# A spectral-MLP stage with its mask products on VectorE and its MLP blocks, sums and transform slots in another order

## The reference

```python
residual = x
xn = _ln(transpose(x, (0, 2, 3, 1)), ln1w, ln1b)          # layer norm over the 64 channels
xf = jnp.fft.rfft2(xn, axes=(1, 2), norm='ortho')
o1r, o1i = relu(complex product of xf with w1 + b1)
o2r, o2i = complex product of (o1r, o1i) with w2 + b2
mask = ((jnp.abs(o2r) > THR) | (jnp.abs(o2i) > THR)).astype(o2r.dtype)
o2r, o2i = o2r * mask, o2i * mask                          # THR = 0.01
x = residual + irfft2(complex(o2r, o2i))
h = gelu(_ln(x, ln2w, ln2b) @ mw1 + mb1, approximate=False)   # 64 -> 256
x = x + (h @ mw2 + mb2)                                    # 256 -> 64
```

## Time and profile before

| | |
|---|---|
| median of 3 runs | 3960.04 us (3946.08 to 3962.07) |
| profiled execution | 3955.85 us, of which the span of instructions 3953.8 us |
| TensorE busy | 3359.4 us (85%) |
| VectorE busy | 2409.8 us (61%) |
| ScalarE busy | 2378.0 us (60%) |
| GpSimd busy | 1706.6 us (43%) |
| mean granted TensorE clock | 0.937 |

### The profile page before, as it was taken

The page is one execution under the profiler, slowest core; times in us unless marked ns, Lnnn a source line. Parts: engine busy times, 40 slices in busy tenths (PEclk is TensorE's granted clock), DMA queues, the critical chain, the costliest instruction groups (busy, mean ns, idle before and its releaser), DMA issues. The chain is left out here.

```text
span 3953.8 us, 54117 instructions
## 1 busy us (share of the span) xinstructions
PE 3359.4 (85%) x18664; PEld 2064.3 (52%) x18664; DVE 2409.8 (61%) x4175; ACT 2378.0 (60%) x3944; POOL 1706.6 (43%) x1397
## 2 busy tenths in 40 slices
PE   2952779999999999898989899999999999967579
PEld 0741646555555556464646464656464646345237
DVE  1834566656565666666666666565756565449567
ACT  0843466656565656576766565665656565637448
POOL 2404444544444444444454545545444443234242
PEclk9975889999999999999999999999999999989879
DMA  9861111101111111212111101010111111163698
GB/s 222 257 223 60 38 48 43 59 27 59 42 45 43 44 49 43 86 65 107 65 66 43 59 28 59 27 64 26 60 38 49 38 49 43 64 237 123 165 276 242
DMA packets 235118, 334.15 MB, mean 85 GB/s; under 512 B 38625, under 2 KB 163681, under 8 KB 228721
## 3 DMA queue, kind: packets, MB, share of 16 engines
q1 hardware_dynamic: 198112, 298.44, 22.2%
q10 hardware_dynamic: 28784, 18.44, 2.0%
q0 software_dynamic: 7968, 13.99, 1.4%
HBM read 183.99 MB, written 146.80 MB: 84 GB/s over the span
## 5 line engine op out<-in xcount | busy, mean ns | idle before, releaser
L1490 ACT ACTIVATE a_hidden<-a_wide,a_up_b 128x1024 f32<-128x1024 f32 x512 | 569.4, 1112 | 168.7 <-PE a_wide L1657 168.7
L1657 PE MATMUL a_wide<-a_yc,a_up_fold 64*128 64x512 f32 x2048 | 587.7, 649 | 45.1 <-ACT a_hidden L1490 40.8
L1668 PE MATMUL a_result<-a_hidden,a_down 128*64 128x512 f32 x2048 | 513.4, 623 | 72.2 <-DVE a_x L1356 72.2
L1252 POOL TENSOR_TENSOR a_y<-a_o,a_mag 128x256 f32<-128x256 f32 (+1 forms) x512 | 362.0, 732 | 424.0 <-DVE a_mag L1345 424.0
L1210 POOL TENSOR_TENSOR a_y<-a_x,a_stat 128x512 f32<-128x512 f32 x256 | 266.6, 1044 | 349.7 <-DVEq L1388 320.8
L1328 DVE TENSOR_TENSOR a_o<-a_bank,a_mix_b 128x512 f32<-128x512 f32 (+1 forms) x272 | 181.6, 668 | 376.9 <-PE a_bank L1614 372.3
L1356 DVE TENSOR_TENSOR a_x<-a_result,a_x 128x512 f32<-128x512 f32 x256 | 176.3, 689 | 339.3 <-PE a_result L1683 337.1
L1632 PEld LDWEIGHTS a_bank<-a_dft_h,a_g 128*128 128x128 f32 x2080 | 285.6, 200 | 175.5 <-issue 115.3
L1647 PE MATMUL a_bank<-a_dft_hi,a_y 128*128 128x128 f32 x2048 | 280.1, 303 | 70.5 <-POOL a_y L1252 70.5
L1614 PEld LDWEIGHTS a_bank<-a_mix,a_o 128*128 128x128 f32 x2080 | 253.9, 192 | 154.7 <-issue 135.8
L1632 PE MATMUL a_bank<-a_dft_h,a_g 128*128 128x128 f32 x2080 | 290.4, 284 | 47.3 <-DVE a_g L1321 47.3
(11 more groups left out here) (189 smaller groups left out, 6359.6 us busy)
## 6 DMA issues: line engine op xcount, KB each, us to landing
a_x<-rows SPq DMA_DIRECT2D x112, 512.0 KB, 4.4
rows<-a_x SPq DMA_DIRECT2D x112, 512.0 KB, 2.9
box_x<-in_x SPq DMA_DIRECT2D x64, 256.0 KB, 4.3
turned<-box_o SPq DMA_DIRECT2D x64, 256.0 KB, 3.7
a_y<-turned SPq DMA_DIRECT2D x16, 1024.0 KB, 11.5
box_x<-rows SPq DMA_DIRECT2D x16, 1024.0 KB, 24.2
turned<-box_work SPq DMA_DIRECT2D x64, 256.0 KB, 2.0
box_x<-turned SPq DMA_DIRECT2D x64, 256.0 KB, 3.9
```

The lines of the kernel that those rows point to most:

```text
L1252: ins = G.tensor_tensor(y[n % 2][:, :, to].rearrange("p c k -> p k c"), o2[:, j % 3, lo:4, r], mask[:, lo:4], ALU.mult)
L1490: A(hidden[:, i % 2, j], wide[:], ACT.Gelu, bias=up_b2[:, l, j:j + 1]).then_inc(s_hid, 1)
L1657: mm = M(wide[:, half * BANK:(half + 1) * BANK], up_fold[cs, l, j * P:(j + 1) * P], yc[cs, i % 2], start=True, stop=True)
L1668: mm = M(result[half * C:(half + 1) * C, :], down[:, l, j, :], hidden[:, i % 2, j, half * BANK:(half + 1) * BANK], start=j == 0, stop=j == ...
```

## The change

1. **Mask products.** `masked` and `spectrum` on GpSimd are gone. VectorE's `masks` keeps the maximum, drops the comparison as an instruction of its own, and multiplies `o2` by `(top > THR)` in `scalar_tensor_tensor` instructions, two for each chunk, written to `y`. `o2` has two buffers in place of three.
2. **MLP order.** `turn_back` writes `turned`, and the residual reads `turned`, so `result` belongs to `mlp_down` alone; `mlp_down` is cut into its two halves, which stand in two places of the quarter and wait for `mlp_delta` of the block before (`s_delta`). `turn` comes later in a quarter but for a block further on (Q + 2 in place of Q + 1), so it waits for `normalise` of Q + 2 and for the residual of Q - 2. ScalarE's `operand` becomes the first thing of its quarter; the squares come after the second slot's part.
3. **Slots.** `REST_SLOTS` 5, 7, 17, 18 become 3, 9, 17, 18; `BACKWARD_SLOT` 43 becomes 44; `NEXT_SLOTS` 47, 48, 51, 53 become 48, 49, 53, 57.
4. **Sums.** In quarter 5 the pair of reductions and the root move from the second slot to the fourth, behind the end of the forward transform.
5. **GpSimd's long operations.** `next_y` of quarter 10 is written a slot later.

```diff
-REST_SLOTS = (5, 7, 17, 18)
-FORWARD_SLOT, SPECTRUM_SLOT, BACKWARD_SLOT = 19, 23, 43
-NEXT_SLOTS = (47, 48, 51, 53)
+REST_SLOTS = (3, 9, 17, 18)
+FORWARD_SLOT, SPECTRUM_SLOT, BACKWARD_SLOT = 19, 23, 44
+NEXT_SLOTS = (48, 49, 53, 57)
...
-        o2 = sb("o2", [P, 3, 4, 2, C])
+        o2 = sb("o2", [P, 2, 4, 2, C])
...
-                def masked(n, j):
-                    before, mask = N_CHUNK * n, mag[:, j % 2, :, 0]
-                    kw, lo = first_kw(j), 1 if j < 2 else 0
-                    pool.wait_ge(s_top, 2 * (before + j + 1))
-                    if j < 2:
-                        ins = G.tensor_tensor(ends[:, 1 - j], o2[:, j % 3, 0], mask[:, 0:1].broadcast_to([P, 2, C]), ALU.mult)
-                    if j > 0:
-                        for r in range(2):
-                            to = slice(r * HALF + kw + lo, r * HALF + kw + 4)
-                            ins = G.tensor_tensor(y[n % 2][:, :, to].rearrange("p c k -> p k c"), o2[:, j % 3, lo:4, r],
-                                                  mask[:, lo:4], ALU.mult)
-                    ins.then_inc(s_masked, 1)
...
                     for s in range(4):
-                        parts(n, q, s, inverse, other, spectrum, other)
+                        parts(n, q, s, inverse, other, other, other)
                         if s == 0 and 0 <= Q + 2 < BLOCKS * RUNS:
                             normalise(Q + 2)
-                        if s in (0, 2) and comes:
+                        late = 1 if q == 10 else 0
+                        if s - late in (0, 2) and comes:
...
                     V.tensor_tensor(top[:, 0:k], top[:, 0:k], mag[:, j % 2, 0:k, 1], ALU.max).then_inc(s_top, 1)
-                    dve.wait_ge(s_top, 2 * (before + j) + 1)
-                    V.tensor_scalar(top[:, 0:k], top[:, 0:k], THR, None, ALU.is_gt).then_inc(s_top, 1)
+                    dve.wait_ge(s_top, before + j + 1)
+                    if j < 2:
+                        ins = V.scalar_tensor_tensor(
+                            out=ends[:, 1 - j], in0=top[:, 0:1].broadcast_to([P, 2, C]), scalar=THR,
+                            in1=o2[:, j % 2, 0], op0=ALU.is_gt, op1=ALU.mult)
+                    if j > 0:
+                        for r in range(2):
+                            to = slice(r * HALF + kw + lo, r * HALF + kw + 4)
+                            ins = V.scalar_tensor_tensor(
+                                out=y[n % 2][:, :, to].rearrange("p c k -> p k c"), in0=top[:, lo:4], scalar=THR,
+                                in1=o2[:, j % 2, lo:4, r], op0=ALU.is_gt, op1=ALU.mult)
+                    ins.then_inc(s_masked, 1)
...
-                    V.tensor_tensor(x[:, row:row + HB], rows(result), x[:, row:row + HB], ALU.add).then_inc(s_res, 1)
+                    V.tensor_tensor(x[:, row:row + HB], rows(turned), x[:, row:row + HB], ALU.add).then_inc(s_res, 1)
...
-                    parts(n, q, 1, inverse, forward, spectrum, backward)
-                    for strip in strips_at(n, q):
-                        sum_up(*strip)
-                    if q % 4 == 1 and FIRST_ROOT <= r < END_ROOT:
-                        root(r)
-                    for s in range(2, 4):
+                    for s in range(1, 4):
                         parts(n, q, s, inverse, forward, spectrum, backward)
+                        if s == (3 if q == 5 else 1):
+                            for strip in strips_at(n, q):
+                                sum_up(*strip)
+                            if q % 4 == 1 and FIRST_ROOT <= r < END_ROOT:
+                                root(r)
...
+                    if 0 <= Q + 1 < BLOCKS * RUNS:
+                        operand(Q + 1)
                     if mlp:
                         gelu(Q, 0)
...
                     parts(n, q, 0, inverse, forward, spectrum, backward)
-                    if 0 <= Q + 1 < BLOCKS * RUNS:
-                        operand(Q + 1)
                     parts(n, q, 0, other, other, magnitude, other)
+                    parts(n, q, 1, inverse, forward, spectrum, backward)
                     for strip in strips_at(n, q):
                         square(*strip)
-                    parts(n, q, 1, inverse, forward, spectrum, backward)
...
-                def mlp_down(i):
+                def mlp_down(i, j):
                     l = layer_of(i // BLOCKS)
-                    pe.wait_ge(s_hid, HC * (i + 1))
+                    pe.wait_ge(s_hid, HC * i + j + 1)
                     if i:
-                        pe.wait_ge(s_res, i)
-                    for j in range(HC):
-                        for half in range(2):
+                        pe.wait_ge(s_delta, i)
+                    for half in range(2):
...
                     if i:
                         pe.wait_ge(s_yc, i)
+                    if i >= 4:
+                        pe.wait_ge(s_res, i - 3)
...
                 def turn_back(i):
                     pe.wait_ge(s_delta, i + 1)
+                    pe.wait_ge(s_yc, min(i + 4, BLOCKS * RUNS))
+                    if i + 4 > BLOCKS * RUNS:
+                        pe.wait_ge(s_res, i)
...
-                    if 0 <= Q + 1 < BLOCKS * RUNS:
-                        turn(Q + 1)
+                    if 0 <= Q - 1 < BLOCKS * RUNS:
+                        mlp_down(Q - 1, 0)
                     parts(n, q, 1, inverse, forward, spectrum, backward)
                     if mlp:
                         mlp_up(Q, 1)
                     parts(n, q, 2, inverse, forward, spectrum, backward)
                     if 0 <= Q - 1 < BLOCKS * RUNS:
-                        mlp_down(Q - 1)
+                        mlp_down(Q - 1, 1)
+                    if 0 <= Q + 2 < BLOCKS * RUNS:
+                        turn(Q + 2)
```

More of the change, by code:

```diff
@@ L1325, in spectrum @@
                         dve.wait_ge(s_mix2, before + j + 1)
-                        if j >= 3:
-                            dve.wait_ge(s_masked, before + j - 2)
-                        V.tensor_tensor(o2[:, j % 3, 0:k].rearrange("p k r c -> p k (r c)"), four(bank[3])[:, 0:k],
+                        if j >= 2:
+                            dve.wait_ge(s_masked, before + j - 1)
+                        V.tensor_tensor(o2[:, j % 2, 0:k].rearrange("p k r c -> p k (r c)"), four(bank[3])[:, 0:k],
                                         mix2_b[:, layer_of(n), None, :].broadcast_to([P, k, P]), ALU.add
@@ L1340, in masks @@
                     before = N_CHUNK * n
-                    k, top = chunk(j), mag[:, j % 2, :, 0]
+                    k, kw, lo, top = chunk(j), first_kw(j), 1 if j < 2 else 0, mag[:, j % 2, :, 0]
                     dve.wait_ge(s_mag, before + j + 1)
                     V.tensor_tensor(top[:, 0:k], top[:, 0:k], mag[:, j % 2, 0:k, 1], ALU.max).then_inc(s_top, 1)
-                    dve.wait_ge(s_top, 2 * (before + j) + 1)
-                    V.tensor_scalar(top[:, 0:k], top[:, 0:k], THR, None, ALU.is_gt).then_inc(s_top, 1)
+                    dve.wait_ge(s_top, before + j + 1)
[10 more added lines that the diff above has]
+                    ins.then_inc(s_masked, 1)
                 def backward(n, i):
@@ L1473, in magnitude @@
                             act.wait_ge(s_masked, before + j - 1)
[L1474 removed]
+                        A(mag[:, j % 2, 0:k], o2[:, j % 2, 0:k], ACT.Abs).then_inc(s_mag, 1)
                 def other(n, i):
@@ L1659, in mlp_up @@
                     mm.then_inc(s_up, 1)
-                def mlp_down(i):
+                def mlp_down(i, j):
                     l = layer_of(i // BLOCKS)
-                    pe.wait_ge(s_hid, HC * (i + 1))
+                    pe.wait_ge(s_hid, HC * i + j + 1)
                     if i:
-                        pe.wait_ge(s_res, i)
-                    for j in range(HC):
-                        for half in range(2):
-                            mm = M(result[half * C:(half + 1) * C, :], down[:, l, j, :],
-                                   hidden[:, i % 2, j, half * BANK:(half + 1) * BANK], start=j == 0, stop=j == HC - 1)
-                    mm.then_inc(s_down, 1)
+                        pe.wait_ge(s_delta, i)
+                    for half in range(2):
+                        mm = M(result[half * C:(half + 1) * C, :], down[:, l, j, :],
+                               hidden[:, i % 2, j, half * BANK:(half + 1) * BANK], start=j == 0, stop=j == HC - 1)
+                    if j == HC - 1:
+                        mm.then_inc(s_down, 1)
                 def turn(i):
```

7 lines of the change are left out of this document (1 added, 6 removed).

## The result

The changed kernel takes 4066.48 us (median of 4 runs, 4065.03 to 4085.36), the kernel before 3958.57 beside it: a ratio of 1.028 [1.026, 1.031]. It is slower by 108 us, 7.2 for each of the 15 runs.

The account below looks back on a forecast made before the run. TensorE's work and gaps bound the AFNO stage. Terms 3.6 - 2.3 + 2.8 - 2.6 gave 1.5 us a run, 23 over 15 runs; after adjustments 3955.85 - 22 = 3934, median 3936 us, range 3795 to 3995.

Parts of the forecast that it names:

- rival A: VectorE and GpSimd in the spectrum: the port conflict hardly bites, 11.1 us a run gained, 3789 us; chance 0.17.
- rival B: Spectrum's end: GpSimd gets between the two products, TensorE's waits gather, three clock drops, 4005 us; chance 0.20.
- rival C: MLP quarters: waits only change places, `turn`'s for `normalise` as dear as the residual's, 3976 us; chance 0.18.
- sums behind the forward transform: Quarter 5: moving reductions and root removes TensorE's 3.0 us wait and a 1.7 clock drop; gain 3.6 a run.
- cut `mlp_down` and MLP waits: MLP quarters: halves of `mlp_down` cost 2.3 us a run, fewer waits and clock drops gain 2.8.
- mask products: Spectrum's end, VectorE's products beside GpSimd's long operations: root to transform back 21.2 us against 20.3, one clock drop; -2.6 a run.
- the credit of 4.1 a run: Old stretch from root to transform back: 1.1 us for an `mlp_up` and 3.0 for slow clock added to its 16.2.
- Two VectorE instructions without a wait between them stay together: Last chunks: GpSimd does not get between a pair of products; three chunks in a row take 16.3 us.
- No wait of TensorE: Spectrum behind the root of quarter 5: GpSimd's row of operations there makes TensorE wait nowhere, size 0.
- Without the port conflict +7: Mask products' term in the spectrum: would be +7 us a run in place of -2.6 without the conflict.
- the 0.9 that I counted for shorter restarts: MLP quarters: blocks start closer together once waits are gone; some 0.9 us a run gained.
- the 1.1 that I took off for late copies and the held group: Forward transform: ScalarE's last copies come late, 0.5 us, and the third forward group is held, 0.6, a run.

Follow-up runs that it names:

- e12: The kernel before with only the reductions and root of quarter 5 moved behind the forward copies; 3869.88 us, ratio 0.976.
- e10: e1 with the slots of the kernel before; 3934.35 us, ratio 0.993.
- e1: The changed kernel with comparison back on VectorE and mask products back on GpSimd, three `o2` buffers; 3964.92 us, ratio 1.003.
- e3: The changed kernel with GpSimd waiting for the last mask product before `next_y` of quarter 10; 3974.32 us, ratio 1.005.
- e5: e2 with GpSimd waiting for the last product before `next_y` of quarter 10; 3868.20 us, ratio 0.976.
- e2: The kernel before with only the mask products moved to VectorE; 4048.07 us, ratio 1.023.
- e6: The changed kernel with the maximum written to PSUM except in chunks 5 to 8, ScalarE's `Abs` in two instructions; 3963.42 us, ratio 1.001.
- run 13: One of the 15 runs inside a profiled execution, compared across kernels; its three stages took 22.8, 76.9, 91.4 us before, 20.7, 83.0, 91.9 changed.
- e7: e3 with ScalarE's squares behind the second GELU outside quarters 4 to 10; 3935.10 us, ratio 0.994.
- e8: e1 with ScalarE's squares behind the second GELU outside quarters 4 to 10; 3928.25 us, ratio 0.992.
- e11: e3 with the slots of the kernel before; 3928.63 us, ratio 0.991.
- e4: The changed kernel with all of ScalarE's squares behind the second GELU of the quarter; 4058.73 us, ratio 1.026.

## Why the prediction was wrong

The time came out above the range. My forecast and rival A were wrong; what happened is the exchange of rival B, waits in the MLP that are as dear as those that went, as in rival C, and one loss that I had in no case (the slots). The experiments make a chain from the kernel before to the change: sums -92 (e12), MLP order +64 (e10 against e12), slots +38 (e1 against e10), products +98 (the change against e1). They add up to 108 by the way they are made; in another order of steps the sizes differ (the products' meeting costs 88 by e3, 186 by e5). e10 also keeps the later slot of `next_y` (part 5 of the change), so the step "MLP order" holds both. Per run, a gain positive:

| term | predicted | measured |
|---|---|---|
| sums behind the forward transform | +3.6 | +6.1 |
| cut `mlp_down` and MLP waits | -2.3 + 2.8 | -4.3 |
| slots | 0 | -2.5 |
| mask products | -2.6 | -6.5 |
| sum | +1.5 | -7.2 |

It helps to put the same steps by stage, in us over the 15 runs, a loss positive. The forecasts are my terms, put where each of them belongs; the measured ones are from the starts in the traces, and leave out some 5 us outside these stages:

| | forward | spectrum | rest |
|---|---|---|---|
| sums | -28, measured -46 | -26, measured -24 | 0, measured -16 |
| MLP order | +2, measured +15 | +11, measured +12 | -19, measured +32 |
| slots | 0, measured -2 | 0, measured 0 | 0, measured +31 |
| products | 0, measured +1 | +101, measured +102 | -61, measured -1 |

The spectrum came out as forecast, and nearly all of the error is in the rest: 80 us of gain forecast, 46 of loss measured. Three steps failed there: the credit of 4.1 a run within the products' term, the gain of the MLP order, and the slots, which I put at nothing.

*Mask products.* The -2.6 was the new stretch from the root to the transform back (21.2, and 1.7 for a clock drop) against 20.3 for the old one: 16.2, 1.1 for an `mlp_up`, and 3.0 for the slow clock behind it. The first number is nearly right (22.3 for 22.9, by the same count). The second is the step that failed: with the products on GpSimd in the new order (e1) the stretch takes 14.6, and the clock does not fall behind it. So the 4.1 was no gain of the products, and they cost 6.5. In e2, on the old order, the credit does not appear either: TensorE waits 3.6 for `o2` and 4.0 for the last product there, with the clock at 0.51 for 7.0 us at each (3019.50 to 3026.50 and 3033.10 to 3040.10), which is rival B as I described it, and the rest stays at 1364.

That the new stretch came out right (3033.04 - 3012.66 = 20.4, predicted 20.6) is luck in part, since what fills it is not what I described. "Two VectorE instructions without a wait between them stay together" was read from one case. The next two operations of VectorE in that same view, of the kernel before, say the opposite:

```profile
3569.50 2.01 DVE L718 TENSOR_SCALAR box_work<-box_work 128x512 f32<-128x512 f32 x1
...
3571.43 2.71 DVE L724 TENSOR_TENSOR box_work<-box_work,box_x 128x512 f32<-128x512 f32 x1
```

They follow each other without a gap and took 2.01 and 2.71, where the same line 724 ran in 1.05 just before; I read each now as sitting out one GpSimd operation. I had taken that earlier row for the rule and read no further. In the changed kernel GpSimd's next operation gets between the two products in the same way: 6.14 and 5.19 for a pair of 1.05, while the maximum beside them runs in 0.64 and 0.42. The Trainium skill ("SBUF — State Buffer", "Who interferes with whom") had it: who starts first keeps the port pair for the whole instruction. The trace agrees, by the rows at 3014.15 and 3021.45, and e6 bears out that a PSUM input in the place of one of the two takes the conflict away. So two chunks were held for 13.9 us (3012.79 to 3026.64) and three followed in 6.4, where I had three in 16.3 and two in 4.3. Beside that:
- TensorE's waits there are 1.4, 3.6 and 0.6, gathered as rival B had it, and the clock is low once, for 6.8 us, where B counted three drops and I one. It adds nothing to the stretch, since VectorE sets that; my 1.7 for it was not due. Against it, the root ended 1.9 later behind the first spectrum step than before (62.6 against 60.7, and 61.7 in e1), where I had 0.56.
- The products take 0.61 alone, not 0.42, so a pair takes 1.05. The same 256 elements cost the maximum 0.42. This lengthened each chunk by about 0.2 and is no large part: e5 wins with it.
- "No wait of TensorE" behind the root of quarter 5 was wrong: the same row of GpSimd operations holds a maximum for 1.99 and the next product for 2.29, and TensorE waits 0.88 at 2970.82.
- "Without the port conflict +7": held clear of `next_y`, the products win 6.2 a run on the kernel before (93 / 15, e5). On the new order they win nothing (e3 is 9 us slower than e1): their waits in the spectrum were only 1.4 + 1.4 there, against the 4.4 of before.

*MLP order.* The halves are as predicted: by the medians of the distances between starts, e10's pairs take 2.02 against 1.87 for a whole one, 2.4 over 16 blocks. The new waits nearly are: 6.2 in `turn` and 0.6 in `turn_back`, predicted 5.4. All of TensorE's waits together were 11.3 in run 13 of e12 and 11.8 in that of e10, so no waiting time was won. The clock drops did go. In the rest of that run of e12 the clock is low twice, at 3.4 us of cost together, and in run 13 of e10 it is 1.00 throughout:

```profile
2865.70:2869.30 3.60, 3.60 (x20) 3.60 (x19) 0.69 (x1) 0.60 (x1) 3.60 (x3) 0.53 0.00 0
...
2937.50:2940.90 3.40, 3.40 (x8) 0.82 (x8) 2.05 (x2) 1.30 (x2) 3.40 (x2) 0.50 0.02 5
```

Yet the run grew by 2.9 (185.3 to 188.2). What ate the gain is the step that failed, the 0.9 that I counted for shorter restarts: the blocks stand further apart instead. Waits and slow clock taken off, the starts of the blocks in the two runs give 2.7 more for the halves in all, 1.0 more for `turn`, 1.4 more for `turn_back`, and 0.5 more for the other blocks; with 0.5 more of waits and 3.4 less of slow clock that is 2.7 of the 2.9. Why these stand further apart is not tried. The mean over all runs is 3.9 by the same starts; what the others add I have not taken apart.

*Slots.* I counted them at nothing and named nothing that covers them. The transform back one slot later puts its last inverse part against the two strips of quarter 12, and the rows at 3060.63 to 3065.27 show the chain; e7, e8, e10 and e11 agree on 38 to 53 us for slots or squares. The slots were only put back all together, so how much of this each of them makes is not shown. That chain crosses three engines (VectorE's addition, ScalarE's square, VectorE's reduction, ScalarE's second square, the GELU) and in the list of before it shows as no more than part of six short waits.

*Sums.* The mechanism was right and the size too small: the 3.0 is gone, 0.2 left, and the clock drop behind it too. In run 13 of e12 the forward transform won 3.0 and the spectrum, where the drop had been, 1.6 (75.3 us), which are my 3.0 and 1.7. What failed is the 1.1 that I took off for late copies and the held group: it doesn't appear. The rest won 1.2 more (90.2). There, behind the same wait of 4.4 for GpSimd's products, the clock is low for 3.6 us (the row at 2865.70 above), against 6 before.

What stays open: why e4 loses as much in the spectrum as it wins elsewhere is read from its waits, not tried; whether one product a chunk, in place of two, would be free of the exchange was not tried.

## What to carry to other kernels

Moving work off an engine also removes the waits that kept that engine's other operations out of the way: ask what will now run early, and beside what. Here one wait of GpSimd for the last product turned +93 us into -93. Before a part is put one slot later, look at what stands in the next slot on *each* engine, above all at single buffers; and try each part of a compound change alone, since two of the parts here (the sums, and the products with GpSimd held) win more without the rest, 3.6% together. Before a gain is credited to one part, ask whether another part brings it anyway: the 4.1 a run that I gave to the products were won by the new order without them.
